# Layer 0's gate and up products by a seven-product scheme, with the down weights' Hadamard product in a bank of its own

## What is computed

```
# layer 0, H = 2048
up_gate = jnp.einsum('bsd,hd->bsh', x, W1)
up_lin = jnp.einsum('bsd,hd->bsh', x, W3)
hidden = jax.nn.silu(up_gate) * up_lin
hidden = fwht(hidden)                     # Walsh-Hadamard over H, times H ** -0.5
out = jnp.einsum('bsh,dh->bsd', hidden, W2)
# layer 1, H = 1408
g = jnp.einsum('th,ih->ti', xf, gate_w) * gate_s
u = jnp.einsum('th,ih->ti', xf, up_w) * up_s
out = jnp.einsum('ti,hi->th', jax.nn.silu(g) * u, down_w) * down_s
```

## Time and profile before

| what | value |
| --- | --- |
| median of 3 runs | 1983.2 us (1976.17 to 1984.47) |
| the profiled execution | 1980.84 us |
| its span on the core | 1978.6 us |
| granted TensorE clock, mean | 0.991 |
| TensorE, VectorE, ScalarE, GpSimd busy | 96%, 59%, 36%, 38% |
| layer 0's output projection | 774.0 to 832.4 us |
| layer 0's feed-forward | 832.4 to 1374.7 us |
| layer 1's output projection | 1551.6 to 1611.1 us |
| layer 1's feed-forward | 1611.1 to 1974.5 us |

### The profile page before, as it was taken

The page is one execution under the profiler, slowest core; times in us unless marked ns, Lnnn a source line. Parts: engine busy times, 40 slices in busy tenths (PEclk is TensorE's granted clock), DMA queues, the critical chain, the costliest instruction groups (busy, mean ns, idle before and its releaser), DMA issues. The chain is left out here.

```text
span 1978.6 us, 26382 instructions
## 1 busy us (share of the span) xinstructions
PE 1897.5 (96%) x9936; PEld 1360.3 (69%) x9936; DVE 1170.3 (59%) x1956; ACT 707.6 (36%) x1275; POOL 759.0 (38%) x722
## 2 busy tenths in 40 slices
PE   7999999999999999899999999999999889998999
PEld 5677555555545545688888888887887567787877
DVE  5466877676666742853434343444432797778776
ACT  4221355555546565421111111113321234334332
POOL 1122678788776589300000000001000615656563
PEclk9999999999999999999999999999999999999999
DMA  9753422322321203110000000002000111111211
GB/s 325 267 152 113 98 55 56 87 54 56 87 44 34 60 12 107 59 43 32 32 2 33 32 23 10 0 20 70 11 6 0 33 32 49 54 54 43 89 57 53
DMA packets 80783, 120.83 MB, mean 61 GB/s; under 512 B 7008, under 2 KB 38768, under 8 KB 80624
## 3 DMA queue, kind: packets, MB, share of 16 engines
q1 hardware_dynamic: 73200, 93.96, 16.6%
q0 software_dynamic: 7456, 25.18, 4.2%
HBM read 93.68 MB, written 25.44 MB: 60 GB/s over the span
## 5 line engine op out<-in xcount | busy, mean ns | idle before, releaser
L1831 DVE TENSOR_REDUCE part_max<-banks 128x1 f32<-128x512 f32 (+2 forms) x640 | 356.9, 614 | 149.1 <-PE banks L1803 90.9
L2356 ACT ACTIVATE probs<-banks 128x512 f32<-128x512 f32 (+3 forms) x640 | 311.1, 538 | 268.7 <-PE banks L2271 133.3
L1803 PE MATMUL banks<-kst,qst 96*128 96x512 f32 (+2 forms) x640 | 261.3, 417 | 12.1 <-DVE part_max L1831 9.6
L2267 PE MATMUL banks<-qst,kst 98*128 98x512 f32 (+2 forms) x640 | 251.2, 412 | 0.7 <-ACT probs L2356 0.7
L1465 POOL TENSOR_TENSOR w_lo<-early_weights,w_hi 128x512 fp32r<-128x512 f32 x4 | 5.1, 1310 | 544.1 <-ACT w_hi L1439 544.1
L763 DVE TENSOR_TENSOR tokens_b<-banks,tokens_b 128x512 f32<-128x512 f32 x64 | 44.3, 692 | 251.7 <-ACT tokens_b L678 251.7
L2217 POOL TENSOR_TENSOR early_weights<-probs 128x512 f32<-128x512 f32 (+2 forms) x152 | 160.5, 1085 | 56.6 <-ACT probs L2356 56.1
L2217 POOL TENSOR_TENSOR pairs_own<-probs 128x512 f32<-128x512 f32 (+2 forms) x152 | 157.2, 1063 | 63.7 <-ACT probs L2356 63.4
L678 ACT ACTIVATE tokens_b<-banks 128x512 f32<-128x512 f32 x64 | 38.3, 598 | 395.6 <-PE banks L229 395.6
L2267 PEld LDWEIGHTS banks<-qst,kst 98*128 98x128 f32 x640 | 123.6, 194 | 64.3 <-issue 49.0
L1803 PEld LDWEIGHTS banks<-kst,qst 96*128 96x128 f32 x640 | 123.5, 193 | 59.9 <-DVE part_max L1831 47.1
(11 more groups left out here) (263 smaller groups left out, 4188.1 us busy)
## 6 DMA issues: line engine op xcount, KB each, us to landing
tokens_a<-in_L_wmod SPq DMA_DIRECT2D x12, 1024.0 KB, 7.3
qst<-q_hi SPq DMA_DIRECT2D x32, 256.0 KB, 6.1
kst<-k_hi SPq DMA_DIRECT2D x32, 256.0 KB, 8.2
tokens_b<-in_down_wt SPq DMA_DIRECT2D x10, 512.0 KB, 3.5
q_hi<-qk_out_hi POOLq DMA_DIRECT2D x16, 256.0 KB, 3.5
q_lo<-qk_out_lo POOLq DMA_DIRECT2D x16, 256.0 KB, 3.4
k_hi<-qk_out_hi POOLq DMA_DIRECT2D x16, 256.0 KB, 3.8
k_lo<-qk_out_lo POOLq DMA_DIRECT2D x16, 256.0 KB, 4.2
```

The costliest lines, as they stand in the source:

```text
L1803: mm = nc.tensor.matmul(dst[:, 0:wide], qst[n % QS][0:BIASROW, h, P * t:P * t + P], kst[(NB * g + c) % KS][0:BIASROW, h, 0:wide], start=Tr ...
L1831: nc.vector.tensor_reduce(part_max[:, n % 2, ht, c:c + 1], max_bank(slot)[:, 0:wide], AX_X, ALU.max).then_inc(max_read, 1)
L2267: mm = nc.tensor.matmul(dst[:, c0:512], kst[ck % KS][0:BIASROW + 2, h, at:at + P], qst[n % QS][0:BIASROW + 2, h, c0:512], start=True, stop ...
L2356: nc.scalar.activation(probs[:, q % PS, h, c0:512], score_bank(sh)[:, c0:512], ACT.Exp, scale=SCALE).then_inc(exp_done, 1)
```

## The change

Layer 0's `feed_forward` and `projection_and_norm` go. Layer 0 uses `winograd_forward` and `projection_and_pairs` too, with 16 chunks: 32 units, 8 segments of two units in each of two passes. For layer 0 (`mixed`, there are no down scales):

- the down weights are multiplied by the gate row on GpSimd before the Hadamard product, split, multiplied by `hadamard` on TensorE into bank 7 (`mix`), and the result is split again, out of that bank, by ScalarE (`mixed_hi`) and VectorE (`mixed_lo`). The two chunks of a segment use bank 7 one after the other. Since each pass goes through all segments, this is done twice per chunk,
- down tiles have the two banks 5 and 6 instead of three,
- hidden values are made in the buffers `gate0` and `gate1`, which frees `act_`,
- the stage's end takes the calls of the next stage (`behind`) in: layer 1's first norm block in unit 29, its transposes ahead of the last 8 down tiles.

For both layers, the down weights of segment 0 are multiplied in unit 1 instead of unit 0; and the semaphores of the seven products are merged into one counter for products made and one for products taken. GpSimd adds layer 0's first weight sums between residual tiles 9 and 10.

```
-                        if c == 0:
+                        if c == (q == 0):
                             Stage.down_gate_gpsimd(pool, q)
...
+            DOWN_BANKS = 2 if mixed else 3
...
+                drow = early_gate
+                made = (gate0, gate1)
...
+            def down_bank(n):
+                return bank[5 + n % DOWN_BANKS]
+
+            def mixes(u, j):
+                q, c = segment(u)
+                if not mixed or u == 0:
+                    return []
+                if u == 1:
+                    return [(0, 0)] if j == 6 else []
+                if u == 2:
+                    return [(0, 1)] if j == 1 else []
+                return [(q, (j - 3) // 2)] if c and j in (3, 5) else []
...
+                        if n >= DOWN_BANKS:
+                            pe.wait_ge(x_added, n - DOWN_BANKS + 1)
...
+                    def mix(q, c):
+                        n = 2 * q + c
+                        pe.wait_ge(m_ready, n + 1)
+                        if n == 0:
+                            pe.wait_ge(norm.h_ready, KT * NB)
+                        else:
+                            pe.wait_ge(d_ready, n)
+                        nc.tensor.matmul(bank[7][:], hadamard[:], dh[:, q % 2, c, :], start=True, stop=False)
+                        nc.tensor.matmul(bank[7][:], hadamard[:], dl[:, q % 2, c, :], start=False, stop=True).then_inc(mix_mm, 1)
...
+                    def mixed_hi(q, c):
+                        act.wait_ge(mix_mm, 2 * q + c + 1)
+                        nc.scalar.copy(dh[:, q % 2, c, :], bank[7][:]).then_inc(d_hi_s, 1)
...
                         if c == (q == 0):
                             down_hi(q)
+                        if mixed and c and q:
+                            mixed_hi(q, 0)
                         hidden_hi(u, 0)
+                        if mixed and c and q:
+                            mixed_hi(q, 1)
+                        if behind and u == UNITS - 3:
+                            behind.ahead_scalar(act)
...
+                    def mixed_lo(q, c):
+                        dve.wait_ge(d_hi_s, 2 * q + c + 1)
+                        nc.vector.tensor_tensor(dl[:, q % 2, c, :], bank[7][:], dh[:, q % 2, c, :],
+                                                ALU.subtract).then_inc(d_ready, 1)
...
                         if u:
                             hidden_lo(u - 1, 1)
+                        if mixed and u == 2:
+                            mixed_lo(0, 0)
                         add_trunk2(u)
                         add_gate1_part(u)
+                        if mixed and u == 2:
+                            mixed_lo(0, 1)
...
                         if c == (q == 0):
                             down_lo(q)
                         add_up0(u)
-                        hidden(u, 0)
+                        if mixed and c and q:
+                            mixed_lo(q, 0)
+                        make_hidden(u, 0)
                         for q, t in last:
                             add_x(q, t)
                         hidden_lo(u, 0)
+                        q, c = segment(u)
+                        if mixed and c and q:
+                            mixed_lo(q, 1)
+                        if behind and u == UNITS - 3:
+                            behind.ahead_vector(dve)
...
             def first_tensor(pe):
-                    pe.wait_ge(before.hidden_made, before.units - 1)
+                    pe.wait_ge(before.products_taken, before.taken_34)
                     norm.tensor(pe, 0)
```

688 lines of the change are left out of this document (188 added, 500 removed).

## The result

The changed kernel takes **2004.8 us** (median of 4 runs, 2003.9 to 2006.9) against 1980.7 (4 runs) of the kernel before on the same chip: ratio **1.0124**, 95% interval 1.0098 to 1.015. It is 1.2% slower; 2005.5 was forecast. The profiled execution took 2006.9 us, its span 2005.1, 26.5 more than the span of before. It is the slowest of the four; by the medians the change costs 24.1 us.

The account below looks back on a forecast made before the run. TensorE, busy 96% of the span, was taken to bound the kernel. -36.3 us of products, +55.6 of waits and +3 in layer 1 gave +22.3 on 1983.2: 2005.5 us, 1.1% slower, range 1982 to 2032.

Parts of the forecast that it names:

- 15 stops before the second Hadamard product: Layer 0, segments 1 to 15: TensorE waits 1.55 us, plus 0.1 for slower matmuls, for `mixed_lo` each time; +24.8 us.
- change of half: Layer 0, where the token half changes: 4.8 us of waits; layer 1 lost 8.0, mostly lateness that other waits now absorb.
- segment 0: Layer 0's first segment: later GpSimd scaling makes Hadamard products and first down tile wait 3.6, 4.8 and 1.6; +10.3 with restarts.
- two down banks: Layer 0, two down banks for three: 0, since VectorE's room makes the needed addition 1 us early.
- layer 1's scaling: Layer 1's first scaling moves to unit 1 too, so `down_lo(0)` ends later: +3 us (0 to 3.4).
- What would show it: Trace signs: 15 waits of 1.5 to 1.8 us released by `mixed_lo`, `add_up0` idle before, layer 0's stage about 564 us.
- The ring as the bound: Rival: the VectorE, GpSimd and ScalarE ring of a unit pair exceeds 32.4 us, waits are 3.0, about 2026; chance 0.22.
- The clock at each wait: Rival: TensorE's clock falls after each of 15 waits, 0.9 us each, +14, about 2019; chance 0.08.
- The covered wait: Rival: TensorE comes late to product 5 and finds bank 7 free, only starts and ends are paid: -2.5; chance 0.12.
- the cheap starts: Rival: segment 0 and the start and end of layer 0's stage at their lower ends, -15: 1990.5; chance 0.18.
- the bank of its own: Layer 0: both Hadamard products write bank 7, so the second waits for `mixed_lo(q, 0)` behind `add_up0`; 15 x 1.65 = +24.8 us.
- The rule that the prediction weighed: A VectorE operation with two SBUF operands and a GpSimd one exclude each other for a whole instruction, lengthening the ring.

Follow-up runs that it names:

- experiment 2: Changed kernel with TensorE's second Hadamard product issued behind product 6 instead of product 5: 1982.0 us, ratio 0.9997 to the kernel before.
- experiment 4: Changed kernel with GpSimd's scaling of segment 0 back in unit 0, in layer 1 alone: 2007.5 us, ratio 1.0130 to the kernel before.
- experiment 12: Changed kernel with three banks in turn, GpSimd's scaling back in unit 0, `mixed_lo(0, 1)` earlier, `mixed_lo(q, 0)` ahead of `add_trunk3`: 1972.6 us, ratio 0.9959 to before.
- experiment 1: Changed kernel with VectorE's `mixed_lo(q, 0)` ahead of `add_up0(u)` instead of behind it: 1991.6 us, ratio 1.0050 to the kernel before.
- experiment 3: Changed kernel with VectorE's `mixed_lo(q, 0)` one operation later, behind `make_hidden(u, 0)`: 2030.2 us, ratio 1.0248 to the kernel before.
- Experiment 6: The kernel of 5 with ScalarE, in unit 15, rounding the first Hadamard product behind the first two new operands: 1975.1 us, ratio 0.9954 to before.
- 8: Changed kernel with two down banks instead of three in layer 1 too: 2013.3 us, ratio 1.0154 to the kernel before.
- 5: Experiment 2's kernel with segment 0 scaled in unit 0, its second Hadamard product in bank 6, `mixed_lo(0, 1)` earlier: 1974.7 us, ratio 0.9967 to before.

## Why the prediction was right, and where its steps were off

The forecast was 2005.5 us and the result 2004.8. That the two agree within 1 us is partly luck: the median of before came out at 1980.7 and not at 1983.2, and the change was forecast as +22.3 where the medians give +24.1 and the spans +26.5, with errors of several us in both directions among the terms. The steps of the sum, with a wait counted as its row plus 0.29 (experiment 2) and slow matmuls at 0.20 each:

| step | forecast | measured |
| --- | --- | --- |
| 160 fewer products | -36.3 | a pair without waits is 136 x 0.2267: holds |
| 15 stops before the second Hadamard product | 24.8 | 13 x 1.76 = 22.9; unit 31 2.6; unit 15 4.7 and 12 slow matmuls, 2.4: 32.5 |
| change of half | 4.8 | 2.7, the rest is unit 15's stop above |
| segment 0 | 10.3 | (1.62 + 4.26 + 1.38) + 0.9, 12 slow matmuls 2.4: 10.5 |
| start, units 0 and 1 | 10.6 | 6.35 + 4 x 0.29, 17 slow matmuls 3.4: 10.9 |
| projection | 8 | 8.8 |
| two down banks | 0 | 0.53 + 1.21 + 0.6: 2.3 |
| norm block in unit 29 | 3.9 | 1.71 + 0.58 + 0.6: 2.9 |
| end | 6.1 | 3.06 + 0.19 + 0.6, 5 slow matmuls and 8 slow transposes 1.6: 5.4 |
| token sums and small gaps | 3 | 2.0, what is left over |
| layer 1's scaling | +3 | stage 0.8 shorter in this execution; some 2 longer over twelve (experiment 4) |

The waits from 774.0 on come to 78.2 us (626.6 less 192 + 2176 products and 80 transposes) where 71.5 were forecast; before it was 15.9. Layer 0 was 6.6 us worse than forecast, layer 1 3.8 better, the stretch between them 1.4 worse. That stretch has the same code in all kernels, and takes between 236.4 and 238.7 us in the fourteen traces, so the 1.4 is within the scatter of executions.

**The central step held.** The wait was read off the order of two queues and the spacing of VectorE's operations. 1.55 + 0.1 was forecast; 1.47 by the row, 1.63 counted as the forecast counts it, and 1.76 by the pair was measured, with `mixed_lo` as the releaser and `add_up0` idle before it, as "What would show it" asked. The experiments moved only that one operation, by one place either way, or the product by one place: pairs of 31.42, 30.83 and 33.54 us followed.

**The rivals.** The ring as the bound is refuted for the steady pairs: 32.59 us a pair fell to 30.83 as soon as the order allowed, with 0 waits. In segments 1 to 3 some of it is left: no edit brought all these pairs to 30.83 (34.13 at most in the changed kernel and 34.16 in experiment 12), and experiment 1 shows GpSimd's sums and ScalarE's roundings as what is late in segments 2 and 3. The clock at each wait is refuted for 1.47 us; experiment 3 shows it for 6 of 13 waits of 2.3 to 2.9. The prediction read only two slow products behind layer 1's wait of 3.99 us; the trace has eight transposes and five matmuls at the lower clock there. The covered wait and the cheap starts didn't come.

**The terms that were off.** First, in "the bank of its own" I priced 15 equal stops. Unit 15's is 3 times as long: ScalarE has five operands of the new half ahead of `mixed_hi(q, 0)`, so `mixed_lo` itself waited 1.39 us. I took the change of half for "lateness that the waits above now absorb". Experiment 6 shows that it is the place of `mixed_hi` in ScalarE's queue. Second, no term held the lower clock behind the long waits. Changed kernel, TensorE at unit 15:

```profile
1107.69 0.76 PE L725 MATMUL banks<-v_d_hi,hadamard 128*128 128x512 f32 x1 [4.37 <-DVE v_d_lo L911]
1108.25 0.63 PE L726 MATMUL banks<-v_d_lo,hadamard 128*128 128x512 f32 x1
...
1112.94 0.52 PE L228 MATMUL banks<-v_b_lo,v_a_hi 128*128 128x512 f32 x1
1113.30 0.39 PE L229 MATMUL banks<-v_b_hi,v_a_lo 128*128 128x512 f32 x1
```

Twelve matmuls in 5.05 us, 0.42 each, where 0.23 is usual. There are five such stretches in layer 0 (behind waits of 2.60, 3.03, 4.26, 4.37 and 3.06 us; 8, 9, 12, 12 and 5 matmuls): 46 x 0.20 = 9 us, against one of 6 matmuls before. How many are slow changes from one execution to the next: behind the same wait of unit 15 (4.37 to 4.39 us) it is 6 to 8 matmuls in experiments 1, 3, 4 and 8, and in all of layer 0 some 36 in experiments 4 and 8, whose layer 0 is the changed kernel's, for 46 here. From 774 us on, it takes 624.9 us in both of these and 626.2 here, so 1.3 us of the 6.6 belong to this one execution. The rule on the repeated fall (the Trainium skill, "TensorE: Matmul & The Clock Gate", section "HAM oscillation — how this bites in real kernels") tells of waits of some 3 to 5 us with a fall at each; here it bore on the few long waits, and the stop of 1.47 us never brought a fall. The longer one of experiment 3, 2.3 to 2.9 us, brought it at about half of the stops, though it is shorter than the page's. Third, errors went the other way: layer 1 came out 3.8 better (by experiment 4 the move of its scaling costs some 2 and not 3; the rest is of the size by which single executions differ), and segment 0's first wait was 1.62 for 3.6 (2.7 and 2.9 in experiments 4 and 8, whose layer 0 is the same). Two banks at "0" was too low even with the stops (3.6 us in four places, 1.71 of them in the table's row of the norm block); without the stops it was 4.9, and in layer 1 they cost 9.8.

**The rule that the prediction weighed.** It found the trace of VectorE beside GpSimd to agree in kind and not in size. In size it agrees as well, as the last point below shows: `make_hidden` is held up until GpSimd's instruction has ended. What was overrated is what such a hold-up costs: in the steady stretches of experiment 2 `make_hidden` takes 1.17 to 1.21 us, and a pair still takes 30.83 us without a wait.

**What the loss is made of**, then, is the hand-over and not the scheme: without Hadamard products the scheme gains 1.5% (0.4 of it for the 32 that before had), with them in the order of the change it loses 1.2%, and with them a place later (2), a better start (5) and half (6) it gains 0.5%; three banks in turn with `mixed_lo` ahead (12) gain 0.4%.

## What to carry to other kernels

When a product's bank is freed by another engine, find in that engine's queue what stands ahead of the freeing operation: if it waits for the product that the waiting engine issued last, a wait is to be expected, whatever the engines' busy shares say, and its price can be added up from the spacing of rows. In this kernel moving one instruction by one place, on either engine, took most or all of it away, which is worth trying before a bank or a buffer is spent on it; the units where a half or a stage changes have other queues and are priced by themselves, slow matmuls behind a long wait included.
